# One-pass products of split tokens and weights in the local attention, and new orders, in a kernel of four streams of layers on one core

## The reference

```python
h = shift_token(x)                 # half of the features come from the token before
qkv = h @ wqkv                     # (256 x 128) @ (128 x 1536), per sequence and layer
q, k, v = jnp.split(qkv, 3, axis=-1)
q = l2norm(q) * qs                 # 8 heads of 64
k = l2norm(k) * ksc
q, k = rotary_xpos(q, k)
o = local_attention(q, k, v)       # windows of 64, each sees itself and the one before
x = x + o @ wo
```

## Time and profile before

| | us |
|---|---|
| median of 3 runs | 2973.64 |
| lowest and highest | 2973.01, 2973.70 |
| span of the profiled execution | 2969.2 |
| busy PE | 2718.0 (92%) |
| busy PE weight loads | 1930.1 (65%) |
| busy DVE | 2338.1 (79%) |
| busy ACT | 2123.2 (72%) |
| busy POOL | 1605.4 (54%) |

### The profile page before, as it was taken

One profiled execution on the slowest core, in us unless ns is written; L12 is line 12 of the kernel. 1 busy time (PEld: TensorE's weight loads), 2 busy tenths in 40 slices (PEclk: granted clock), 3 DMA queues, 4 the chain that ended last, 5 costly groups with the idle time before them and its releaser, 6 DMA issues.

```text
span 2969.2 us, 66891 instructions
## 1 busy us (share of the span) xinstructions
PE 2718.0 (92%) x23144; PEld 1930.1 (65%) x23144; DVE 2338.1 (79%) x5888; ACT 2123.2 (72%) x5956; POOL 1605.4 (54%) x1747
## 2 busy tenths in 40 slices
PE   5778999999999999999999999999999999999887
PEld 3455666666666666666666666666766666666665
DVE  3467778888888888888888888888888888887764
ACT  2356687778778777777877777777777777777663
POOL 1035455565556556555655665565566555556653
PEclk8889999999999999999999999999999999999989
DMA  2000000000000000000000000000000000000000
GB/s 71 3 3 4 5 5 6 5 6 7 7 7 5 6 5 6 6 7 7 5 6 5 7 6 7 7 5 6 5 7 6 7 7 5 6 7 5 5 3 8
DMA packets 41978, 21.83 MB, mean 7 GB/s; under 512 B 21130, under 2 KB 41012, under 8 KB 41652
## 3 DMA queue, kind: packets, MB, share of 16 engines
q1 hardware_dynamic: 41652, 17.55, 2.1%
HBM read 9.17 MB, written 4.19 MB: 5 GB/s over the span
## 4 chain that ended last, share of the span: by engine, by line
PE 54%; ACT 25%; DVE 16%; issue 2%; POOL 2%; DMA 0%; SPq 0%; DVEq 0%; POOLq 0%; ACTq 0%
PE bank L1161 8%; DVE negmax L893 7%; PE bank L1067 6%; ACT P L785 5%; ACT probs L753 5%; PE bank L1229 4%; PE bank L1172 4%; PE bank L1126 3%; PE bank L1194 3%; PE bank L1237 3%; PE bank L1221 3%; ACT rawP L785 3%; PE bank L1086 3%; PE bank L1023 2%; PE bank L1105 2%
## 5 line engine op out<-in xcount | busy, mean ns | idle before, releaser
L753 ACT ACTIVATE probs<-bank 128x512 f32<-128x512 f32 (+1 forms) x1024 | 478.5, 570 | 204.9 <-PE bank L1105 204.1
L893 DVE TENSOR_REDUCE negmax<-bank 128x2 f32<-128x512 f32 (+1 forms) x896 | 554.5, 682 | 51.7 <-PE bank L1086 45.9
L1161 PE MATMUL bank<-wqkv_sb,hS 128*128 128x512 f32 x768 | 400.2, 624 | 24.0 <-ACT rawA L790 12.1
L685 POOL TENSOR_TENSOR rn<-ss_kept,minus_half 128x16 f32<-128x16 f32 x128 | 372.5, 2910 | 65.1 <-DVE ss_kept L953 62.3
L630 POOL TENSOR_TENSOR veps<-moments,eps_tile 128x2 f32<-128x2 f32 x192 | 38.6, 201 | 640.9 <-DVE moments L845 639.8
L652 POOL TENSOR_SCALAR_AFFINE_SELECT probs<-probs 128x256 f32<-128x256 f32 x512 | 199.9, 411 | 235.9 <-ACT probs L753 235.6
L1126 PE MATMUL bank<-probs,V 128*16 128x256 f32 (+1 forms) x4096 | 246.4, 358 | 25.4 <-POOL probs L652 18.5
L973 DVE TENSOR_REDUCE negmax<-bank 128x2 f32<-128x384 f32 (+1 forms) x384 | 206.9, 594 | 37.7 <-PE bank L1194 37.7
L673 POOL TENSOR_TENSOR rawA<-rawA,rope_sb 128x512 f32<-128x512 f32 x128 | 186.4, 1456 | 90.3 <-ACT rawA L772 90.2
L673 POOL TENSOR_TENSOR rawB<-rawB,rope_sb 128x512 f32<-128x512 f32 x128 | 177.4, 1386 | 86.0 <-ACT rawB L772 86.0
L785 ACT ACTIVATE P<-bank,negmax 128x192 f32<-128x192 f32 x512 | 208.3, 454 | 5.9 <-DVE negmax L973 3.8
(11 more groups left out here) (140 smaller groups left out, 7295.7 us busy)
## 6 DMA issues: line engine op xcount, KB each, us to landing
xin<-x SPq DMA_DIRECT2D x32, 128.0 KB, 2.1
out<-xout SPq DMA_DIRECT2D x32, 128.0 KB, 1.8
feed_h<-YB SPq DMA_DIRECT2D x64, 63.5 KB
wqkv_sb<-wqkv SPq DMA_DIRECT2D x1, 1536.0 KB
feed_h<-YB SPq DMA_DIRECT2D x64, 0.2 KB
w_sb<-w SPq DMA_DIRECT2D x1, 682.0 KB
w_sb<-w SPq DMA_DIRECT2D x2, 256.0 KB, 3.2
wo_sb<-wo SPq DMA_DIRECT2D x2, 256.0 KB
```

What stands on the lines that cost most here:

```text
L685: nc.gpsimd.tensor_tensor(rn[:, l, t].rearrange("p m h -> p (m h)"), ss_kept[:, l, t].rearrange("p m h -> p (m h)"), minus_half[:], ALU.po ...
L753: nc.scalar.activation(dst, src, ACT.Exp, scale=SCALE0 if k == ATTN0 else SCALE1)\
L893: nc.vector.reduce_max(negmax[:, k, t, head:head + 4 * many - 3:4], tile(u, e)[:, :].rearrange("p (h k) -> p h k", h=many), AX.X, negate=T ...
L1161: mm(tile(u)[:], hS[:, l, t * P:(t + 1) * P], wqkv2_sb[:, l, m * INNER:(m + 1) * INNER], start=True, stop=True).then_inc(has_filled(u), 1)
```

## The change

1. The weights `wqkv2` are no longer used as they are. They are loaded into two tiles that are free at the start (`rawP` and `kT2`), ScalarE rounds them to float32r (`wqkv2_hi`), and VectorE subtracts to get the rest (`wqkv2_lo`). `staged` now counts to 10 instead of 8.
2. The shifted tokens are split likewise: ScalarE writes `hS_hi` in float32r, and VectorE then subtracts it from the bank to get `hS_lo`. The bank is now emptied by VectorE.
3. A unit `qkv2` is three float32r matmuls that add up in the bank: high by high, high by low, low by high.
4. GpSimd clears two tiles instead of one.
5. `STEADY_FILLERS` has 6 fillers a turn instead of 11, at other units, and `END_FILLERS` has others.
6. All orders and banks are new. `FIRST`, `TURNS` and `LAST` keep their lengths. The streams stand to each other as before to within a few units, but units of different streams alternate more often.

The diff without most of the digits:

```diff
 TURNS = {
     "tensor": (
-        "3333002222200001210102222101201123333311003033333331330113113002222111113333330031133303444422232222"
-        "22221111301401244022222220422132300003305555505550250001233"
+        "3134300252222333000021333302231012530321120131033432030133310131130203333322230101222521511333134310"
+        "32222112213102142202215402220422500154253020334003020025101"
     ),
...
-STEADY_FILLERS = {(ATTN0, "scores", 1): (3, 0), (ATTN0, "maxes", 1): (3, 1), (ATTN1, "scores", 0): (3, 0), (LOCAL0, "qkv2", 0): (2, 0)}
+STEADY_FILLERS = {(LOCAL0, "shift", 0): (3, 0), (LOCAL1, "turn_p", 0): (3, 0)}
 END_FILLERS = {
-    (0, ATTN0): {("turn_q", 0): 5, ("mix", 0): 7, ("mix", 1): 7, ("mix", 2): 7, ("mix", 3): 7, ("turn", 0): 8},
-    (1, ATTN0): {("turn_q", 0): 5, ("mix", 0): 7, ("mix", 1): 3, ("mix", 2): 7, ("turn", 0): 8},
-    (31, LOCAL1): {("qkv2", 2): 9, ("turn_p", 0): 10},
-    (31, FEED1): {("turn", 0): 28},
+    (0, ATTN0): {("mix", 0): 6, ("mix", 1): 6, ("mix", 3): 5},
+    (1, ATTN0): {("maxes", 1): 5, ("maxes", 3): 5},
+    (30, LOCAL0): {("shift", 0): 5, ("scores2", 1): 5},
+    (31, LOCAL0): {("shift", 0): 5},
+    (30, FEED1): {("turn", 0): 7},
+    (31, LOCAL1): {("turn_q2", 0): 8, ("turn_p", 0): 9},
+    (31, FEED1): {("turn", 0): 11},
 }
...
-    units = [Unit("shift", bank=1)]
+    units = [Unit("shift", bank=1, hi_ready=1)]
...
+        wqkv2_in = [raw[:, :, :].rearrange("p l n -> p (l n)")[:, 0:3 * INNER] for raw in
+                    (rawP, kT2[:, :, :, :].rearrange("p l c q -> p l (c q)"))]
...
-            load(wqkv2_sb[:], wqkv2.rearrange("l k n -> k l n"))
+            for l in range(LAYERS):
+                load(wqkv2_in[l], wqkv2[l])
...
-                nc.gpsimd.memset(hS[:], 0.0).then_inc(setup_pool, 1)
+                nc.gpsimd.memset(hS_hi[:].bitcast(f32), 0.0).then_inc(setup_pool, 1)
+                nc.gpsimd.memset(hS_lo[:].bitcast(f32), 0.0).then_inc(setup_pool, 1)
...
                 act.wait_ge(loaded[REST], ALL_LOADED[REST])
+                for l in range(LAYERS):
+                    nc.scalar.activation(wqkv2_hi[:, l], wqkv2_in[l], ACT.Copy).then_inc(rounded, 1)
                 act.wait_ge(setup_pool, PRESETS[REST])
...
-                    nc.scalar.activation(hS[0:64, l, 0:SEQ], src[0:64, 0:SEQ], ACT.Copy)
-                    nc.scalar.activation(hS[64:128, l, 1:SEQ + 1], src[64:128, 0:SEQ], ACT.Copy)\
-                        .then_inc(has_emptied(u), 1)
+                    nc.scalar.activation(hS_hi[0:64, l, 0:SEQ], src[0:64, 0:SEQ], ACT.Copy)
+                    nc.scalar.activation(hS_hi[64:128, l, 1:SEQ + 1], src[64:128, 0:SEQ], ACT.Copy)\
+                        .then_inc(sig("hi_ready", u), 1)
...
                 for l in range(LAYERS):
+                    dve.wait_ge(rounded, l + 1)
+                    nc.vector.tensor_tensor(wqkv2_lo[:, l], wqkv2_in[l], wqkv2_hi[:, l].bitcast(f32), ALU.subtract).then_inc(staged, 1)
...
+                elif u.kind == "shift":
+                    dve.wait_ge(sig("hi_ready", u), so_far("hi_ready", u) + 1)
+                    for rows, at in ((slice(0, 64), 0), (slice(64, 128), 1)):
+                        last = nc.vector.tensor_tensor(hS_lo[rows, l, at:at + SEQ], tile(u)[rows, 0:SEQ],
+                                                       hS_hi[rows, l, at:at + SEQ].bitcast(f32), ALU.subtract)
+                    last.then_inc(has_emptied(u), 1)
...
-                    mm(tile(u)[:], hS[:, l, t * P:(t + 1) * P], wqkv2_sb[:, l, m * INNER:(m + 1) * INNER],
-                       start=True, stop=True).then_inc(has_filled(u), 1)
+                    for n, (tokens, weights) in enumerate(((hS_hi, wqkv2_hi), (hS_hi, wqkv2_lo), (hS_lo, wqkv2_hi))):
+                        last = mm(tile(u)[:], tokens[:, l, t * P:(t + 1) * P], weights[:, l, m * INNER:(m + 1) * INNER],
+                                  start=n == 0, stop=n == 2)
+                    last.then_inc(has_filled(u), 1)
```

More of the change, by code:

```diff
@@ L99 @@
+        "2222111221222222222222000000000000000000000000000000000111111111111111111111111144412222222222222222"
+        "2222222222112212222222222224444400000000000000000000000000033300000333333333303111111111113331131133"
+        "1144111111111422222222222222222222222222112212222222222554444422000000000000000000000000005000003333"
+        "3333333333333333333055555333111111111222222224"
     ),
@@ L131 @@
     "tensor": (
[L132 to L136, removed]
@@ L137 @@
-        "55555115"
+        "3334120032332523320020305310322101233032112003113233003313051131113003131523333242222010213323113223"
+        "3024121131220212222420124240502025021540532030303231320453314331332233122532335112223221123313123331"
+        "3113111332533313342222122435133321211332221131221214224152224222124425355133323233331512233222321211"
+        "2324323251123333131235333513113113323333232124432323231223234222432222244552232552252233332542332234"
+        "3553223333425323232233332222333333334333343333344343335333335333333533533335333333333535335333333333"
@@ L138 @@
+        "55555555"
     ),
     "scalar": (
[L140 to L144, removed]
@@ L145 @@
-        "12233455"
+        "2333002222244302031303001305213201233231311133001310432132030013513321311033323310222201233132323142"
+        "5112125012230202022024240224501225523005130033123213231133223331233224312031312253223114313131333111"
+        "2231332333313241222232131331534522312221511521224422222254423223525143353121243312351132232221332313"
+        "1553252223111333143333131331212332333332113345222233334212222224434544332422452222522225233332322232"
+        "3322233233333222233333333333453233333354335334453523333333335333355335333533333333535533334333533333"
@@ L146 @@
+        "55555353"
     ),
     "vector": (
[L148 to L152, removed]
+        "1300222322302130221300333352233301003311200123031334110113434111030132133120102322233323013133234221"
@@ L153 @@
+        "1203220121222525120251220204424001450550032510332332321331153333322322311320232221231211333213341331"
+        "4341113131231132223322233133331315242212123521222252125412224414253552132253333221533323221113313323"
+        "3322222223331131332311411343141131323322233223332432332352223222224455425423525225225233233325223332"
+        "3233232333322222233325343334443333333433334333434335533333335335353333333533333335333333335353333335"
         "55555555"
@@ L178 @@
-    "27161235647131067574014356204"
+    "3350741657176502317210332526107521612353406537121506514026601751346571265057506531321405016357136731"
+    "4025762345210776430175701603541320615742360352614370563471325047673706124760734650345172610174652301"
+    "4523076123642054633706145230310345107236105423503172304617354712063575630274516372563041703543612770"
+    "3671504675201420153406734206534716234502764103574023261362760240675032157407461537064213075213612045"
+    "7361754230317651243651072374520531074256130714602753427135076243176542047465713207614205371462530147"
@@ L593, in fused_block @@
         ALL_LOADED = [16 * n for n in N_LOADS]
-        PRESETS = [7, 15]
+        PRESETS = [7, 16]
         CLEARED = NBANKS
```

108 lines of the change are left out of this document (51 added, 57 removed).

## The result

The changed kernel takes 3464.14 us (median of 4 runs, 3460.01 to 3482.89) and the kernel before 2973.67: a ratio of 1.1659, 95% interval 1.1639 to 1.1679. It is 16.6% slower where 2.8% faster was forecast, and outside the range. One of the four runs of the kernel before took 5704.99 us, far off the other three (2973.01 to 2973.70), and the ratio leaves it out.

The account below looks back on a forecast made before the run. TensorE's own work was taken to set most of a turn. -2.9 us a turn makes -75 for 26 turns, ends -8, 4.4 outside the span: 2969.2 - 75 - 8 + 4.4 = 2890.6 us, range 2815 to 2985.

Parts of the forecast that it names:

- What bounds the kernel: Repeated turns of 86.31 us: TensorE, busy 82.30, sets most; work taken off it shortens a turn nearly one for one.
- The new orders: Waits in the repeated turns under the rewritten unit orders: 0.0 us a turn, bounds -2.9 and +2.5, besides -0.5 for turn_q.
- three signs of being wrong: TensorE idle above 5 us a turn, granted clock dropping in the turns, or ends moving by more than 20 us.
- -0.5 for `turn_q` of ATTN0: In a turn, a product placed before the first attention's turned heads removes TensorE's 0.55 us wait: -0.5 us.
- The products: The 12 products of a turn, 0.74 us each instead of 0.91: -2.0 us a turn, from -2.8 to a loss of 0.6.
- The rival on weight loads: Rival (2): the products' weight loads show, 0.96 us a product, turn 86.0 us, 2963 us in all; chance 0.13.
- Fillers: Fillers of a turn, eleven become six: 1.6 us less busy, half counted, -0.8 us a turn, bounds 0 and 1.6.
- The low part: Tokens' low part in a turn: VectorE's four subtractions, 1.3 us in spare time; added TensorE wait +0.4, bounds 0 and 1.8.
- rival (4): The clock falls in the turns with fewer fillers and less array work; at 0.95, +6 us a turn, 3050 us; chance 0.06.
- Rival (6): New waits in the more finely interleaved order outweigh the saving: turn 86.4 to 89 us, 2976 to 3040 us; chance 0.03.
- The ends: Start and drain outside the turns: -8 us in sum; their rewritten orders 0, bounds -30 and +15.
- The weights' low part: At the start, VectorE's two subtractions for the split weights, 1.8 us each, 3.6 in all, which TensorE waits for.

Follow-up runs that it names:

- after_both_late: Changed kernel, in its turns both feed-forwards' statistics later on VectorE and GpSimd, FEED1's transposition and first product later too: 3220.15 us, ratio 1.0846.
- before_early_stats: Kernel before, in its turns VectorE takes both feed-forwards' statistics 1 and 2 units behind the row-shift DMAs, not 11 and 19: 3312.22 us, ratio 1.1154.
- products alone: Changed kernel with orders, banks and fillers of the kernel before (one digit of the draining order differs): 3335.06 us, ratio 1.1216.
- orders alone: Kernel before, float32 products kept, with the orders, banks and fillers of the changed kernel: 3444.15 us, ratio 1.1584.
- products_shift_early: Changed kernel with the earlier orders, banks and fillers, but VectorE doing its part of both token shifts earlier in the turns: 3074.46 us, ratio 1.0352.
- shift_earlier: Split products in the earlier orders, VectorE's shifts brought forward, LOCAL1's shift then moved earlier still on TensorE and VectorE: 3060.23 us, ratio 1.0295.

## Why the prediction was wrong

**What bounds the kernel: wrong in its use.** A turn's length was read rightly, and TensorE is its main load. But "work taken off TensorE should shorten a turn nearly one for one" took the waits of before as a property of the kernel. They were one of its order: a transfer that lands 5.9 us after its issue was hidden by 10 and 18 units, so no wait of a turn showed it. It did stand in the trace of before, at the very end, where nothing is left to hide it (the chain, and VectorE's timeline):

```profile
2949.07 5.37 DMA feed_h<-YB
...
2954.46 0.49 DVE L841 BATCH_NORM_STATS2 bn<-feed_h 128x6 f32<-128x128 f32 x2 [5.78 <-DMA feed_h<-YB]
```

**The new orders: the step that failed.** "I take 0.0 with bounds -2.9 [...] and +2.5 (as many waits again)" bounds new waits by the waits that the trace shows. A new order can uncover any latency of the program, not only those already seen. What was missing is the distance from the issue of each DMA to its first user. That distance could be read from the digits, and the length of the transfer from the two rows above. The runs put in its place: TensorE idle 17.8 us a turn, where 4.0 and the bound of 2.5 make 6.5. Of the 490 us, 388 go without the transfer, and 244 with the statistics and FEED1's turn moved back. All three signs of being wrong that the prediction names came with it: idle time above 5 us a turn, a lower clock in the turns, and ends that move by more than 20 us.

The -0.5 for `turn_q` of ATTN0 came true where it was placed: behind four heads and a product it starts without a wait.

```profile
1232.13 0.40 PE L1182 MATMUL bank<-wqkv_hi,hS_lo 128*128 128x512 f32 x1
1232.38 1.09 PE L1087 MATMUL bank<-ident_r,QB 128*128 128x128 f32 x8
```

But the same wait for `KB` came up in ATTN1, whose `turn_q` now stands 7 units behind its projection instead of 22: 2.18 us at 1289.61, the `KB` row under `after_both_late`. It is the same fault once more, a hand-over that the old order hid.

**The products: right in kind, smaller in size.** Forecast -2.0 a turn; measured -1.6 in the old order (0.78 a product on average instead of 0.74: the load of the first instruction shows 0.1 us, not 0.06). In the new order, where a product often follows other work singly, the 12 keep TensorE 10.5 us instead of 11.0 (start to next start, or to its own end where TensorE then idles, in the turn of `after_both_late`): -0.4. The rival on weight loads stays unfit: second and third instruction come 0.23 us apart with loads of the same 128 rows each. The Trainium skill, "TensorE: Matmul & The Clock Gate", section "The mechanism", lets loads overlap only for another row group or into a spare weight buffer; the rows fit the second case, and I had quoted the first alone.

**Fillers: the number right, its worth open.** Six a turn are 1.9 us busy instead of 3.6, so 1.7 went where 1.6 was reckoned. Whether half of that would have shortened the turn can't be seen under the long waits.

**The low part: right in the new order, wrong in the old.** VectorE's four take 1.7 us (forecast 1.3). The wait for it was forecast at 0.4 us a turn, at LOCAL0. In the turn of the changed kernel shown above TensorE doesn't wait for it at all; once the statistics are moved back, 0.7 us a turn show, at LOCAL0 as forecast and nowhere else. In the old order the wait is 8.0 us, far over my bound of 1.8: I had added up durations and not looked where the shift stands on VectorE. Bringing it forward there gave 261 us back, so the split products do need an order of their own.

**The clock: rival (4), on another ground.** I gave it 0.06, "in a turn no idle piece is above 1 us". It fell because the idle pieces became 4 us, not because fillers went: `before_early_stats` keeps all 11 fillers, and its turn of 99.3 us has a clock of 0.95 too, while `after_both_late` has the six and mostly 1.00. In the turn of the changed kernel shown above the clock stands at 0.50 from 1199.8 to 1206.4 us and from 1261.2 to 1264.4, around and behind its two long waits. Its share is 2 to 4 us a turn there: busy 84.39 us at 0.95 against 80.64 at 1.00. Rival (6), new waits, had the mechanism and a chance of 0.03; its dearest turn was 89 us, 2.7 above before, and it came out at 15.9 above.

**The ends: wrong.** Forecast -8. The weights' low part takes 3.3 us at the start (69.56 to 72.90 on VectorE, line 824; forecast 3.6), and the one tile more that GpSimd clears 0.53 us (the 0.5 of the prediction stood in no row); TensorE's first work of sequence 1 starts at 78.60 instead of 73.51, 5.1 us later. But up to the turns 22 us are lost and from the last four turns on 113, of which four turns of +16.1 are 64; so about 70 us lie in the ends. Most of that is the same transfer: outside the 25 turns between the last 26 loads of tokens the changed kernel loses 88 us, and without the transfer 14. No run changed the ends' orders alone, so where in them the statistics should stand is open.

**Open.** That turns of different content came out at 99.0 or 102.4 us (products alone and `before_early_stats` at 99; orders alone and the full change at 102.4) fits waits and falls of the clock that repeat in step with the turn, but no run tested it. In `after_both_late` TensorE's busy time fell by 1.7 us, and the shares of products and fillers (0.4 and 1.7) are 2.1; small transpositions that now stand singly give some back.

## What to carry to other kernels

When a change reorders queues, list every transfer and every cross-engine hand-over with its latency and count what lies between issue and first use in the old and the new order; the waits that a trace shows are only those that the old order fails to hide. Price a split product with its hand-over (here 1.4 us longer, on two engines), and put it where the engine in the middle comes to it at once. Look for these latencies at the start and the end of the trace, where little work hides them. Then look at the clock behind the wait: here a wait of 1.3 us cost as much again in half-speed work, and fillers in it paid for themselves.

## What the runs showed of the hardware

The row shift from SBUF to SBUF moves 63.5 KB in rows of 256 bytes and takes 5.94 us from issue to use, 11 GB/s; at the end of the kernel before it took 5.37. The Trainium skill, "DMA: Bandwidth & Descriptors", section "Anatomy of one DMA", gives a fit for GpSimd's path of 2.0 us and bytes over 436 GB/s, which would be an estimate of 2.15 us here; on this queue of SyncE it took nearly three times as long.

The granted clock went to half for 3.4 us behind the wait of 1.33 us of `products_shift_early`, and for 6.8 us in products alone, from within its wait of 3.55 us on:

```profile
1428.30:1435.10 6.80, 4.22 (x14) 3.53 (x15) 4.35 (x11) 2.24 (x5) 1.36 (x2) 0.50 0.00 1
```

Whether a fall comes depends on more than the longest wait: in `after_both_late` one of 2.2 us passed at full clock in 19 of 25 turns. Within one kernel, a turn at 0.98 took 1.4 to 1.6 us more than one at 1.00 (`products_shift_early`, `shift_earlier`), and one at 0.96 some 3 us more (`products_shift_early`, `after_both_late`).
